# A macaron block on one core: the expert work of two more tiles moved behind the attention, and another chunk closed last

## The chip, the cores and the metric

The kernel runs on one core of a Trainium2 chip (trn2). The metric is the device time of one execution in microseconds. Every time below comes from the runs, from the page of one profiled execution or from its trace, whose clock starts at the first instruction.

## The reference

The input is `x`, 2048 rows of 128 float32 numbers. It goes through a feed-forward part, an attention part and the same feed-forward part again:

```python
x = x + 0.5 * ffn(layernorm(x))
x = x + attn(layernorm(x))        # 16 heads of 8, pages of 32 rows, causal by page, rope
x = x + 0.5 * ffn(layernorm(x))

def ffn(x):                       # L, N = 128, 16; eight experts, capacity 256 rows each
    y1 = ln(x + mha(x, ...), g1, b1)
    y2 = ln(y1 + moe(y1, ...), g2, b2)
    return y2

def moe(x):                       # softmax gate, best expert, rows beyond the capacity dropped
    h = einsum('ecd,edf->ecf', disp, w1) + b1
    y = einsum('ecf,efd->ecd', h, w2) + b2
    out = where(keep, gate_val * y[slot], 0)
```

There is no function between `w1` and `w2`, so the kernel folds each expert into one 128x128 matrix and applies all eight to every row; a coefficient per row and expert (the gate, or 0) picks the right one.

## The kernel before

**Tiles and chunks.** The 2048 rows are 16 tiles of 128 rows, in 4 chunks of 4 tiles. The engines are TensorE (PE), VectorE (DVE), ScalarE (ACT), GpSimd (POOL) and SyncE (SP). Every engine has its own instruction list, and semaphores (`wait_ge`, `then_inc`) tie them together. Nothing is scheduled by a planner: the order on each engine is written out by hand as words such as `P3` or `E10`, a step and the chunk or tile it is for.

**The steps of the second feed-forward part**, which the change is about: `O` adds the projected attention output to the rows and, with `X`, takes their statistics; `A` turns the rows; `P` multiplies them and takes the statistics of y1; `M` normalises y1 (DVE, L879); `C` turns y1 on PE and scales it on ACT and, in rows, on POOL (L545); `L` makes the gate's logits; `R` picks the expert (DVE, L794 to L813; PE, L1137 to L1141); `K` makes the coefficients (DVE, L820 to L823) and turns them; `B` adds a bias row (POOL L509, PE L1152, DVE L833). A letter with 0 to 3 is for a chunk.

**The expert step `E`** is for one tile, 0 to 15. PE makes two products of 512 columns, the high four experts and the low four (L1156, "two halves" below). ACT scales the high one (L673), DVE scales the low one and adds the high (L844, four instructions), and POOL adds the eight parts up in three instructions (L520, L525, L529). For tiles 14 and 15 the first of those three is on DVE (L851). PE may start the low half of tile t only when DVE has finished tile t - 2, since both use one bank:

```python
if t >= 2:
    pe.wait_ge(high_ready, k - 1)
experts(n, t, 1, t % 2)
if t >= 2:
    pe.wait_ge(pair_ready, k - 1)
experts(n, t, 0, 2 + t % 2)
```

**Closing a chunk.** `Z` takes the statistics of y2 (DVE L754 to L762, POOL L501), `V` normalises it on POOL (L535), `F` multiplies by the gain and adds the rows (for chunks 0 to 2 on POOL, `close`, L550 and L553; for chunk 3 on DVE, L958 and L965, four instructions each). SP then stores the chunk (L490).

**Early work.** The attention runs in 16 blocks (a chunk and four heads each). In it ACT does nothing but exponentials (L722), and PE does scores (L1325) and their products with the values (L1347). The steps of chunks 0 to 2 are threaded into these blocks by `PLAN`: `E8@12` in block 14 means the low half of tile 8 behind group 12 of that block, and `H8` is its high half, which DVE scales in place of ACT (L1041). `EARLY_POOL` is POOL's order for this. What is not in `PLAN` stands in the second entry of `ORDER`, and runs behind the last block: this is "the tail".

**Idle work.** `IDLE_WORK` puts products of a constant (L1162), whose result nobody reads, in front of a step on PE: `"C3": (0, 26)` is 26 of them ahead of `C3`.

Of the kernel before, what the change touches and what calls it, by code (L numbers as in the profile page):

```python
# [83 lines left out]
class Pass:  # L84
# [20 lines left out]
}  # L105
# [6 lines left out]
EARLY_POOL = ("X0 B0 P0 M0 C0 X1 B1 E0 P1 M1 C1 E1 E2 E3 Z0 V0 F0 X2 B2 E4 E5 P2 M2 C2 E6 E7 Z1 V1 F1 "  # L112
              "E8 E9")

# [21 lines left out]
    {  # L136
# [4 lines left out]
    },  # L141
# [3 lines left out]
START_WORK = 20  # L145
IDLE_WORK = {"C0": (12, 0), "O3": (0, 4), "A3": (0, 3), "C3": (0, 26), "L3": (0, 4),
             "K3": (0, 2), "B3": (0, 1)}
# [7 lines left out]
def build(nc, a, out):  # L155
    with ExitStack() as ctx:
# [52 lines left out]
        def rows(k):  # L209
# [115 lines left out]
        def group(g):  # L325
            return slice(GT * g, GT * (g + 1))
# [37 lines left out]
        def _(sp):  # L364
# [87 lines left out]
            with sp.If(beyond_safe > 0):  # L452
# [34 lines left out]
                sp.wait_ge(shift_out, 16 * 2 * G)  # L487
            for g in range(G):
                sp.wait_ge(x_new[2], g + 1)
                sp.dma_start(out[cols(g), :].rearrange("(t p) d -> p t d", p=P),  # L490
                             x_tm[:, GT * g:GT * (g + 1), :]).then_inc(stored, 16)
# [4 lines left out]
        def _(pool):  # L496
# [50 lines left out]
            def close(g):  # L547

                pool.wait_ge(normed[LN2], EARLY + g + 1)
                pool.tensor_tensor(y[:, group(g), :], y[:, group(g), :], rows_of(lnb[:, 0, :]), ALU.mult).then_inc(z_part, 1)  # L550
                pool.wait_ge(z_part, G + g + 1)
                pool.wait_ge(xb_ready, G + g + 1)
                pool.tensor_tensor(x_tm[:, group(g), :], y[:, group(g), :], xb[1][:, group(g), :],  # L553
                                   ALU.add).then_inc(x_new[2], 1)

# [3 lines left out]
            def feed_forward(n):  # L559
                for step, g in steps(n, "pool"):  # L560
# [10 lines left out]
                    elif step == "F":  # L571
                        close(g)
                    elif step == "D":

                        pool.wait_ge(const_in, 16 * SMALL)
                        pool.tensor_scalar(lnb[:], lnb[:], 0.5, None, ALU.mult).then_inc(prep_pool, 1)
                        pool.wait_ge(prep_pool, 2)
                    elif step == "B":
                        add_bias(n, g)
                    elif step == "b":  # L580
                        pool.wait_ge(b1_ready, 1)
                        pool.wait_ge(fold_in, 16 * FOLD)
# [165 lines left out]
        def _(dve):  # L748
# [108 lines left out]
            def feed_forward(n):  # L857
                for step, g in steps(n, "dve"):
# [87 lines left out]
                    elif step == "F":  # L946
# [7 lines left out]
                        else:  # L954
# [565 lines left out]
```

## Time and profile before

| | |
|---|---|
| median of 3 runs | 419.14 us (417.70 to 419.77) |
| the profiled execution | 418.99 us |
| its span in the trace, first to last instruction | 417.1 us |
| PE busy | 385.8 us (92%) |
| ACT busy | 325.8 us (78%) |
| DVE busy | 193.3 us (46%) |
| POOL busy | 129.4 us (31%) |
| exponentials of the attention on ACT (L722) | 253.4 us in 272 instructions |
| last exponential ends, tail begins | 381.1 us |
| last result instruction on DVE ends | 414.4 us |

The first 120 us are the first feed-forward part and the preparation of the attention, from 120 to 381 us the attention runs, and the rest is the tail. In the rows a time is the start from the beginning of the span, then the length in us, the engine, the line of the kernel and the operation with what it writes and reads; "x4" counts the instructions merged into the row; square brackets hold the idle time of the engine ahead of it and what ended it.

### The profile page before, as it was taken

The page shows a single profiled execution, that of the slowest core. Times are in us where ns is not written, and L with a number is a line of the kernel's source. Part 1 is how long each engine was busy: PE and PEld are TensorE (multiplying, and loading weights), DVE is VectorE, ACT ScalarE, POOL GpSimd, SP SyncE. Part 2 cuts the span into 40 slices and gives each one's busy share as a digit, 9 for nine tenths or more (in the row PEclk, how much of TensorE's full clock was granted, in tenths as well). Part 3 has the DMA queues.
Part 4 walks back from the last instruction along what each step waited for, and adds up shares of the span by engine and source line. Part 5 has one row for each costly group of instructions (what it writes and reads, how often), then busy time and mean ns, then how long its engine had stood idle before and what let it go on. Part 6 is the DMA issues. An engine that isn't in the chain of part 4 may idle for free.

```text
span 417.1 us, 7529 instructions
## 1 busy us (share of the span) xinstructions
PE 385.8 (92%) x2700; PEld 130.1 (31%) x2704; DVE 193.3 (46%) x729; ACT 325.8 (78%) x466; POOL 129.4 (31%) x203
## 2 busy tenths in 40 slices
PE   6889999789879999999999999999999999999991
PEld 3577443234322233222222222222222222213440
DVE  3866589799862333214242232261332421312856
ACT  1244556566789999999999999999999999996141
POOL 1372788673120023000302210063122330110594
PEclk9999999989988999999999999999999999999997
DMA  6891900000995399600000000000000000000001
GB/s 134 269 349 46 141 2 2 0 1 0 258 255 104 99 194 254 113 2 2 2 2 0 2 0 2 2 0 28 2 1 2 2 25 2 1 2 2 1 25 30
DMA packets 17758, 24.54 MB, mean 59 GB/s; under 512 B 2616, under 2 KB 14584, under 8 KB 16632
## 3 DMA queue, kind: packets, MB, share of 16 engines
q1 hardware_dynamic: 17428, 23.91, 23.9%
q8 instruction: 23, 0.38, 0.4%
q0 software_dynamic: 288, 0.10, 0.2%
q14 instruction: 19, 0.16, 0.1%
HBM read 16.60 MB, written 7.41 MB: 58 GB/s over the span
## 4 chain that ended last, share of the span: by engine, by line
PE 52%; ACT 15%; DVE 12%; issue 10%; DMA 4%; POOL 4%; SPq 1%; ACTq 0%; DVEq 0%; POOLq 0%
PE ps L1347 21%; ACT arena L722 13%; PE ps L1325 12%; PE ps L1156 8%; DVE stats L754 2%; PE ps L1094 2%; DVE arena L844 2%; DMA packed<-piece_dram 2%; PE ps L1110 2%; PE ps L1204 1%; PE ps L1130 1%; DMA x_tm<-in_x 1%; PE ps L1152 1%; DMA piece_dram<-packed 1%; POOL arena L520 1%
## 5 line engine op out<-in xcount | busy, mean ns | idle before, releaser
L722 ACT ACTIVATE arena<-ps 128x1024 f32<-128x1024 f32 x272 | 253.4, 1072 | 7.7 <-PE ps L1325 6.7
L1347 PE MATMUL ps<-arena,v_st 128*9 128x512 f32 (+3 forms) x1280 | 145.3, 536 | 0.1
L1325 PE MATMUL ps<-packed 51*128 51x512 bf16 (+4 forms) x640 | 94.5, 354 | 6.3 <-ACT arena L722 2.2
L501 POOL TENSOR_TENSOR rstd<-var_eps,neg_half 128x4 f32<-128x4 f32 x28 | 28.5, 1017 | 145.8 <-DVE var_eps L762 145.8
L1325 PEld LDWEIGHTS ps<-packed 51*128 51x128 bf16 (+1 forms) x640 | 23.8, 94 | 110.9 <-ACT arena L722 99.3
L1347 PEld LDWEIGHTS ps<-arena,v_st 128*9 128x9 f32 x1280 | 20.7, 89 | 52.6 <-issue 37.4
L520 POOL TENSOR_TENSOR arena<-trio 128x256 f32<-128x256 f32 x14 | 10.2, 726 | 86.7 <-DVE trio L844 86.7
L1156 PE MATMUL ps<-w,arena 128*128 128x512 f32 x64 | 31.0, 611 | 4.1 <-DVE arena L844 4.0
L1156 PE MATMUL ps<-w,trio 128*128 128x512 f32 x64 | 33.9, 629 | 0.0
L844 DVE SCALAR_TENSOR_TENSOR trio<-ps,arena,trio 128x128 f32<-128x128 f32 x64 | 18.0, 344 | 33.9 <-PE ps L1156 31.8
L989 DVE STREAM_TRANSPOSE o_t<-ps 128x512 f32<-128x512 f32 x16 | 11.5, 717 | 40.3 <-PE ps L1347 40.3
L673 ACT ACTIVATE arena<-ps,arena 128x128 f32<-128x128 f32 x64 | 17.9, 368 | 12.8 <-PE ps L1156 7.6
L1041 DVE TENSOR_SCALAR trio<-ps,arena 128x128 f32<-128x128 f32 x40 | 11.3, 345 | 26.1 <-PE ps L1156 26.1
L1162 PE MATMUL ps<-idle 128*128 128x512 bf16 x74 | 18.9, 400 | 2.8 <-DVE idle L973 2.5
L844 DVE SCALAR_TENSOR_TENSOR arena<-ps,arena 128x128 f32<-128x128 f32 x64 | 17.5, 342 | 3.5 <-ACT arena L673 1.9
L632 ACT ACTIVATE arena<-arena,offset,rstd 128x128 f32<-128x128 f32 x28 | 11.5, 484 | 9.7 <-POOL offset L504 9.7
L638 ACT ACTIVATE trio<-ps 128x512 f32<-128x512 f32 x9 | 5.4, 596 | 17.0 <-PE ps L1110 15.4
L1156 PEld LDWEIGHTS ps<-w,arena 128*128 128x128 f32 x64 | 10.9, 189 | 20.1 <-issue 10.3
L1156 PEld LDWEIGHTS ps<-w,trio 128*128 128x128 f32 x64 | 10.1, 188 | 21.7 <-issue 20.9
L545 POOL TENSOR_TENSOR arena<-arena,g_rep 128x512 f32<-128x512 f32 x8 | 10.1, 1272 | 21.7 <-PE ps L1110 21.7
L525 POOL TENSOR_TENSOR arena<-arena 128x128 f32<-128x128 f32 x32 | 15.7, 490 | 2.9 <-DVE arena L851 0.5
L529 POOL TENSOR_TENSOR arena<-arena 128x128 f32<-128x128 f32 x32 | 15.5, 483 | 2.5
(146 smaller groups left out, 404.9 us busy)
## 6 DMA issues: line engine op xcount, KB each, us to landing
packed<-piece_dram SPq DMA_DIRECT2D x16, 384.0 KB, 6.8
piece_dram<-packed SPq DMA_DIRECT2D x18, 256.0 KB, 4.0
packed<-in_w1T SPq DMA_DIRECT2D x8, 256.0 KB, 5.1
packed<-in_w SPq DMA_DIRECT2D x8, 256.0 KB, 5.5
trio<-in_rope SPq DMA_DIRECT2D x2, 1024.0 KB, 6.9
piece_dram<-trio SPq DMA_DIRECT2D x6, 256.0 KB, 9.8
packed<-in_template SPq DMA_DIRECT2D x2, 720.0 KB, 12.5
x_tm<-in_x SPq DMA_DIRECT2D x4, 256.0 KB, 5.8
```

Of the source, the lines that this page charges most:

```text
L501: pool.tensor_tensor(rstd[:, t], var_eps[:, t], neg_half[:], ALU.pow).then_inc(ln_rstd[kind], 1)
L520: pool.tensor_tensor(q, pair[n][:, t % 2, 0:2 * D], pair[n][:, t % 2, 2 * D:4 * D], ALU.add).then_inc(quad_ready, 1)
L525: pool.tensor_tensor(q[:, 0:D], q[:, 0:D], q[:, D:2 * D], ALU.add).then_inc(quad_ready, 1)
L529: pool.tensor_tensor(y[:, t, :], q[:, 0:D], base[:, t % (2 * GT), :], ALU.add).then_inc(z_ready, 1)
L632: ins = nc.scalar.activation(dst[:, t, :], src[:, t, :], ACT.Identity, bias=offset[:, t:t + 1], scale=rstd[:, t:t + 1])
L673: ins = nc.scalar.activation(prod[n][:, t % 2, cut], ps[:, t % 2, cut], ACT.Copy, scale=coef[n][:, t, e:e + 1])
L722: nc.scalar.activation(pexp[:, n % PB, :], ps[:, at:at + 2, :].rearrange("p b n -> p (b n)"), ACT.Exp, scale=SCALE).then_inc(run.exp_done, 1)
L844: ins = dve.scalar_tensor_tensor(pair[n][:, t % 2, D * e:D * (e + 1)], ps[:, bank, D * e:D * (e + 1)], coef[n][:, t, e:e + 1], prod[n][:, ...
L1156: pe.matmul(ps[:, bank, :], y1T[n][:, P * t:P * (t + 1)], w12[:, 512 * high:512 * (high + 1)], start=True, stop=True).then_inc(high_mm if ...
L1162: pe.matmul(ps[:, bank, :], idle[:, 0:P], idle[:], start=True, stop=True)
L1325: ins = pe.matmul(ps[:, 2 * (n % SLOTS) + b, col:col + w], tile_of(rows, 1, pair, j), packed[rows, c, 0, pair, q - GW * c:q - GW * c + w], ...
L1347: ins = pe.matmul(ps[32 * h:32 * h + VW, 6 + k % OB, q - GW * c:q - GW * c + w], v_st[:, j, GH * g + h, :], pexp[:, n % PB, 512 * b + col: ...
```

## The change

1. The four words `H8 E8 H9 E9` leave `PLAN`, and `E8 E9` leave `EARLY_POOL`. Tiles 8 and 9 get their expert work in the tail, whose orders are rewritten on PE, ACT, DVE and POOL. `E10` and `E11` are now ahead of `C3` on PE, and 12 idle products stand there in place of 26.
2. In the tail DVE takes the statistics `Z2` behind `K3` (it was behind `M3`), and POOL does `Z2 V2` behind `B3` (it was ahead of it).
3. POOL does `F2`, the closing of chunk 2, as its very last step; SP stores the chunks in the order 0, 1, 3, 2, the last one behind a semaphore `closing` of its own.
4. POOL waits for y1 of chunk 3 to be normalised (`M3`) before it adds up tile 9.

All lines of the functions move down by up to 7 (L1156 is L1163, L879 is L886).

```diff
@@ PLAN, EARLY_POOL
-    14: "Z1@0 L2@1 S2@5 R2@5 K2@7 B2@8 H8@10 E8@12", 15: "H9@1 E9@3",
+    14: "Z1@0 L2@1 S2@5 R2@5 K2@7 B2@8",
...
-              "E8 E9")
+              )
@@ ORDER, the tail
-        "pe": "E10 O3 A3 E11 P3 C3 L3 E12 R3 K3 E13 B3 E14 E15",
-        "act": "E10 A3 E11 C3 L3 K3 E12 E13 E14 E15",
-        "dve": "O3 X3 E10 P3 E11 M3 Z2 L3 R3 K3 E12 B3 E13 E14 E15 Z3 F3",
-        "pool": "X3 E10 P3 E11 C3 Z2 V2 F2 B3 E12 E13 E14 E15 Z3",
+        "pe": "E8 O3 A3 E9 P3 E10 E11 C3 L3 E12 R3 K3 E13 B3 E14 E15",
+        "act": "E8 A3 E9 E10 E11 C3 L3 K3 E12 E13 E14 E15",
+        "dve": "O3 X3 E8 P3 E9 M3 E10 E11 L3 R3 K3 Z2 E12 B3 E13 E14 E15 Z3 F3",
+        "pool": "X3 E8 P3 E9 E10 C3 E11 B3 Z2 V2 E12 E13 E14 E15 Z3 F2",
@@ IDLE_WORK
-IDLE_WORK = {"C0": (12, 0), "O3": (0, 4), "A3": (0, 3), "C3": (0, 26), "L3": (0, 4),
+IDLE_WORK = {"C0": (12, 0), "O3": (0, 4), "A3": (0, 3), "C3": (0, 12), "L3": (0, 4),
@@ SP
-            for g in range(G):
-                sp.wait_ge(x_new[2], g + 1)
+            for g in (0, 1, G - 1, EARLY - 1):
+                if g == EARLY - 1:
+                    sp.wait_ge(closing, 2)
+                else:
+                    sp.wait_ge(x_new[2], min(g, 2) + 1)
@@ POOL, close
+                part, at, closed = (closing, 1, closing) if g == EARLY - 1 else (z_part, G + g + 1, x_new[2])
                 pool.wait_ge(normed[LN2], EARLY + g + 1)
-                pool.tensor_tensor(y[:, group(g), :], y[:, group(g), :], rows_of(lnb[:, 0, :]), ALU.mult).then_inc(z_part, 1)
-                pool.wait_ge(z_part, G + g + 1)
+                pool.tensor_tensor(y[:, group(g), :], y[:, group(g), :], rows_of(lnb[:, 0, :]), ALU.mult).then_inc(part, 1)
+                pool.wait_ge(part, at)
@@ POOL, feed_forward
+                        if n and g == 9:
+                            pool.wait_ge(normed[LN1], 2 * G)
                         add_experts(n, g)
@@ DVE, F of the last chunk
-                            dve.wait_ge(z_part, q + 1)
+                            dve.wait_ge(z_part, q + 1 - n)
```

PE in the tail, from `P3` to `C3`, before: `P3` (L1094) is followed by the idle products and the turning of y1 (L1110).

```order
L1156 MATMUL ps<-w12,trio 128x512 [waits high_ready]
L1156 MATMUL ps<-w12,trio 128x512 [waits pair_ready]
L1094 MATMUL ps<-w_mha,trio 128x128 [waits copied_rows]
L1094 MATMUL ps<-w_mha,trio 128x128 x3
L1162 MATMUL ps<-idle 128x512 x26
L1110 MATMUL ps<-ident,arena 128x128 [waits normed_ln1]
```

The same place now:

```order
L1163 MATMUL ps<-w12,trio 128x512 [waits high_ready]
L1163 MATMUL ps<-w12,trio 128x512 [waits pair_ready]
L1101 MATMUL ps<-w_mha,trio 128x128 [waits copied_rows]
L1101 MATMUL ps<-w_mha,trio 128x128 x3
L1163 MATMUL ps<-w12,trio 128x512 [waits high_ready]
L1163 MATMUL ps<-w12,trio 128x512 [waits pair_ready]
L1163 MATMUL ps<-w12,trio 128x512 [waits high_ready]
L1163 MATMUL ps<-w12,trio 128x512 [waits pair_ready]
L1169 MATMUL ps<-idle 128x512 x12
L1117 MATMUL ps<-ident,arena 128x128 [waits normed_ln1]
```

The two halves ahead of `P3` are those of tile 9 (they were those of tile 11), and those of tiles 10 and 11 came in behind it; each half has its wait.

POOL in the tail, behind `C3`, before: `Z2` (L501, L504), `V2` (L535), `F2` (L550, L553), `B3` (L509), then tile 12.

```order
L545 TENSOR_TENSOR arena<-arena,g_rep 128x512 [waits turned_y1,normed_ln1]
L501 TENSOR_TENSOR rstd<-var_eps,neg_half 128x4 [waits ln_var_ln2]
L504 TENSOR_TENSOR offset<-neg_mean,rstd 128x4 [waits ln_rstd_ln2]
L535 TENSOR_SCALAR arena<-arena,rstd,offset 128x128 [waits ln_offset_ln2]
L535 TENSOR_SCALAR arena<-arena,rstd,offset 128x128 x3
L550 TENSOR_TENSOR arena<-arena,lnb 128x512 [waits normed_ln2]
L553 TENSOR_TENSOR x_tm<-arena 128x512 [waits xb_ready,z_part]
L509 TENSOR_TENSOR arena<-x_tm,lnb 128x512 [waits x_new_attn]
L520 TENSOR_TENSOR arena<-trio 128x256 [waits z_ready,pair_ready]
```

The same place now:

```order
L549 TENSOR_TENSOR arena<-arena,g_rep 128x512 [waits turned_y1,normed_ln1]
L524 TENSOR_TENSOR arena<-trio 128x256 [waits z_ready,pair_ready]
L529 TENSOR_TENSOR arena<-arena 128x128 [waits quad_ready]
L533 TENSOR_TENSOR arena<-arena 128x128 [waits quad_ready]
L513 TENSOR_TENSOR arena<-x_tm,lnb 128x512 [waits x_new_attn]
L505 TENSOR_TENSOR rstd<-var_eps,neg_half 128x4 [waits ln_var_ln2]
L508 TENSOR_TENSOR offset<-neg_mean,rstd 128x4 [waits ln_rstd_ln2]
L539 TENSOR_SCALAR arena<-arena,rstd,offset 128x128 [waits ln_offset_ln2]
L539 TENSOR_SCALAR arena<-arena,rstd,offset 128x128 x3
L524 TENSOR_TENSOR arena<-trio 128x256 [waits z_ready,pair_ready]
```

Tile 11 and `B3` now come ahead of `Z2 V2`, and `F2` is gone from here.

The end of POOL's list now (before, it ended with the first row but two, L501 there):

```order
L529 TENSOR_TENSOR arena<-arena 128x128 [waits last_quad]
L533 TENSOR_TENSOR arena<-arena 128x128 [waits quad_ready]
L505 TENSOR_TENSOR rstd<-var_eps,neg_half 128x4 [waits ln_var_ln2]
L555 TENSOR_TENSOR arena<-arena,lnb 128x512 [waits normed_ln2]
L558 TENSOR_TENSOR x_tm<-arena 128x512 [waits xb_ready,closing]
```

The two instructions of `F2` stand behind `Z3` (L505), which is what DVE's own last four instructions wait for.

## Rows read from the trace of the kernel before

**Rows 1.** The page, costliest groups: the exponentials on ACT.

```profile
L722 ACT ACTIVATE arena<-ps 128x1024 f32<-128x1024 f32 x272 | 253.4, 1072 | 7.7 <-PE ps L1325 6.7
```

**Rows 2.** Timeline of ACT, 318 to 381 us, the last two attention blocks.

```profile
350.60 3.77 ACT L722 ACTIVATE arena<-ps 128x1024 f32<-128x1024 f32 x4 [0.31 <-PE ps L1325]
354.69 10.38 ACT L722 ACTIVATE arena<-ps 128x1024 f32<-128x1024 f32 x11 [0.32 <-PE ps L1325]
365.39 15.69 ACT L722 ACTIVATE arena<-ps 128x1024 f32<-128x1024 f32 x17 [0.31 <-PE ps L1325]
```

**Rows 3.** Timeline of PE, 376 to 417 us, the tail.

```profile
386.69 1.88 PE L1156 MATMUL ps<-w,trio 128*128 128x512 f32 x4
388.41 1.05 PE L1094 MATMUL ps<-w_mha,trio 128*128 128x128 f32 x8
389.30 5.78 PE L1162 MATMUL ps<-idle 128*128 128x512 bf16 x25
395.49 0.66 PE L1110 MATMUL ps<-ident,arena 128*128 128x128 f32 x4 [0.41 <-DVE arena L879]
...
399.92 0.18 PE L1137 MATMUL ps<-pick_bf,tri_bf 128*128 128x32 bf16 x1
```

**Rows 4.** Timeline of DVE, 376 to 417 us, the tail.

```profile
390.67 0.87 DVE L754 BATCH_NORM_STATS2 stats<-arena 128x6 f32<-128x128 f32 x4
...
392.13 1.12 DVE L844 SCALAR_TENSOR_TENSOR trio<-ps,arena,trio 128x128 f32<-128x128 f32 x4
393.36 2.08 DVE L879 TENSOR_SCALAR arena<-arena,mv,rstd 128x128 f32<-128x128 f32 x4
...
399.57 0.20 DVE L811 TENSOR_TENSOR pick_bf<-arena,row_pick 128x32 bf16<-128x32 f32 x1
...
400.73 0.20 DVE L823 TENSOR_TENSOR arena<-pick,gate 128x32 f32<-128x32 f32 x1
402.86 1.13 DVE L844 SCALAR_TENSOR_TENSOR trio<-ps,arena,trio 128x128 f32<-128x128 f32 x4 [1.93 <-ACT trio L673]
...
413.25 1.14 DVE L965 SCALAR_TENSOR_TENSOR x_tm<-arena,rstd 128x128 f32<-128x128 f32 x4 [0.18 <-DVE arena L958]
```

**Rows 5.** Timeline of POOL, 376 to 417 us, the tail.

```profile
393.55 0.73 POOL L520 TENSOR_TENSOR arena<-trio 128x256 f32<-128x256 f32 x1
...
396.30 1.27 POOL L545 TENSOR_TENSOR arena<-arena,g_rep 128x512 f32<-128x512 f32 x1 [0.94 <-PE ps L1110]
...
399.13 1.76 POOL L535 TENSOR_SCALAR arena<-arena,rstd,offset 128x128 f32<-128x128 f32 x4
400.98 1.26 POOL L550 TENSOR_TENSOR arena<-arena,lnb 128x512 f32<-128x512 f32 x1
...
403.55 1.26 POOL L509 TENSOR_TENSOR arena<-x_tm,lnb 128x512 f32<-128x512 f32 x1
404.77 0.72 POOL L520 TENSOR_TENSOR arena<-trio 128x256 f32<-128x256 f32 x1
...
406.52 0.72 POOL L520 TENSOR_TENSOR arena<-trio 128x256 f32<-128x256 f32 x1
...
410.57 0.45 POOL L529 TENSOR_TENSOR arena<-arena 128x128 f32<-128x128 f32 x1
412.11 1.05 POOL L501 TENSOR_TENSOR rstd<-var_eps,neg_half 128x4 f32<-128x4 f32 x1 [1.09 <-DVE var_eps L762]
```

**Rows 6.** Timelines of POOL and DVE, 335 to 338 us: a large and a small instruction together.

```profile
336.17 1.27 POOL L553 TENSOR_TENSOR x_tm<-arena 128x512 f32<-128x512 f32 x1
...
336.48 1.01 DVE L811 TENSOR_TENSOR pick_bf<-arena,row_pick 128x32 bf16<-128x32 f32 x1
```

**Rows 7.** DMA issues, 400 to 417 us: the two last stores, KB each, us to landing.

```profile
out_rows<-x_tm SPq DMA_DIRECT2D x2, 256.0 KB, 2.3
```

**Rows 8.** Busy time by stretch: PE, PEld, DVE, ACT, POOL, then PEclk, DMA share, GB/s.

```profile
80.00:82.00 2.00, 0.11 (x1) 0.00 (x0) 1.93 (x13) 0.00 (x0) 0.21 (x1) 1.00 0.00 0
...
84.00:86.00 2.00, 1.48 (x3) 0.37 (x2) 2.00 (x7) 0.86 (x3) 1.92 (x3) 0.50 0.00 0
```

More of the change, by code:

```diff
@@ L276, in build @@
         wo_in = sem("wo_in")
+        closing = sem("closing")
         const_in, mha_in, route_in, fold_in, att_in, rope_in, template_in = (sem(n) for n in
@@ L547, in close @@
             def close(g):
+                part, at, closed = (closing, 1, closing) if g == EARLY - 1 else (z_part, G + g + 1, x_new[2])
                 pool.wait_ge(normed[LN2], EARLY + g + 1)
-                pool.tensor_tensor(y[:, group(g), :], y[:, group(g), :], rows_of(lnb[:, 0, :]), ALU.mult).then_inc(z_part, 1)
-                pool.wait_ge(z_part, G + g + 1)
+                pool.tensor_tensor(y[:, group(g), :], y[:, group(g), :], rows_of(lnb[:, 0, :]), ALU.mult).then_inc(part, 1)
+                pool.wait_ge(part, at)
                 pool.wait_ge(xb_ready, G + g + 1)
                 pool.tensor_tensor(x_tm[:, group(g), :], y[:, group(g), :], xb[1][:, group(g), :],
-                                   ALU.add).then_inc(x_new[2], 1)
+                                   ALU.add).then_inc(closed, 1)
             pool.memset(neg_half[:], -0.5).then_inc(prep_pool, 1)
```

## The prediction

> **What bounds the kernel now.** I read the page first, for the engine that is busy longest, then the timeline of ACT through the attention, then the timelines of PE, DVE and POOL in the tail side by side. The attention belongs to ACT: its 272 exponentials are 253.4 us, and it stands idle for 7.7 us in all, nearly always for a score product of PE [rows 1]. The reader is to see that ACT never waits long, but a little at a time, behind each piece of early work on PE [rows 2]. The tail is another kernel: no engine is full, and what counts is one chain through them. PE multiplies (`P3`), DVE takes statistics and normalises, PE turns y1 as soon as DVE is done (395.49, idle until L879) [rows 3], and so on to the last adds on POOL and DVE's last four instructions [rows 4, 5]. I make the sum against the profiled execution, 418.99 us, which is 0.15 us under the median of 419.14 us. A difference of 0.5%, 2.1 us, is about what a measurement of this kernel can tell from none.
>
> **1. Four expert halves leave the attention: -1.6 us.** ACT's free pace is that of its last run, 17 exponentials in 15.69 us, the last of them 1.07 long: (15.69 - 1.07) / 16 = 0.91 us each. The four from 350.60 to 354.69 took 4.09 us in place of 3.64, 0.45 lost; the eleven from there to 365.39 took 10.70 in place of 10.01, 0.69 lost [rows 2]. The idle gap ahead of 350.60 is like the one ahead of 354.69, 0.45 again. These are exactly the places of `H8`, `E8`, `H9` and `E9`: 1.6 us. Bounds: 1.2 us (the four idle gaps alone, at 0.31) and 1.9.
>
> **2. The same work in the tail is hidden in itself.** Tile 8 and 9 stand where tiles 10 and 11 stood. Tiles 10 and 11 are 2 x 1.88 us on PE (the row at 386.69) [rows 3] in place of 14 of the 26 idle products; on DVE they are 2 x 1.1 us where `Z2` stood. `Z2`, 1.5 us (390.67 to 392.13) [rows 4], goes into the 1.93 us in which DVE waited for ACT (402.86) [rows 4]. That costs nothing as long as the waits fit, and one doesn't.
>
> **3. `C3` comes late: +1.3 us.** PE may start the low half of tile 11 only when DVE has finished tile 9, and DVE does tile 9 behind `P3`, in the slot that ends at 393.25 (392.13 + 1.12) [rows 4]. PE gets there long before: it begins the last pass of `P3` at about 389.2 and three halves are 3 x 0.86, so it stands from about 392.1 to 393.3. Then come the low half, 0.9, and 12 idle products at 0.22 (5.78 us for about 26 [rows 3]), 2.6 us: PE can turn y1 at 396.8, not at 395.5. Queued behind that wait on PE are `C3`, `L3` and all that follows. DVE's normalising will be faster, since POOL's adds no longer run beside it: four instructions took 2.08 us beside them (393.36 and 393.55) [rows 4, 5], and four instructions of that size by themselves, L844, take 1.12. It ends between 394.2 and 394.5, I take 394.2, and I count the gain at nothing, because PE is not ready before 396.8.
>
> **4. DVE's pick meets POOL: +0.85 us.** One row shows what a long POOL add does to a small DVE instruction with two inputs in SBUF: L811, 0.20 us when free [rows 4], took 1.01 us and ended just behind POOL's L553 [rows 6]. POOL in the tail now does three tiles and `C3` on end from 394.2: 3 x 1.75 (404.77 to 406.52) [rows 5] + 1.27 = 6.5 us, so `B3`, 1.26 us (403.55) [rows 5], runs from 400.7 to 402.0. DVE's L811 is due at 399.57 + 1.3 = 400.9, inside it. It will end at 402.1 and not at 401.1. PE had 0.15 us to spare there (tile 12 held it until 399.92 [rows 3]), so 0.85 us go through. Bounds: 0, if POOL is 0.4 us later than I have it, and 1.2.
>
> The Trainium skill, "SBUF — State Buffer", section "Who interferes with whom", says that DVE with two SBUF inputs and GpSimd reading SBUF exclude each other for a whole instruction; that row agrees. By its rule the DVE instructions of the expert step, with one input in PSUM, are untouched.
>
> **5. The last adds: +0.3 us.** `K3` ends on DVE at 400.93 + 2.15 = 403.1, then `Z2` until 404.6, POOL's `Z2 V2` 3.1 us (1.05 at 412.11 and 1.76 at 399.13 [rows 5], and 0.3 for the small one and the gaps) until 407.8, then tiles 12 and 13 at 1.75 and 14 and 15 at 1.0: 413.3. Tile 15 ended at 411.02 before (410.57 + 0.45) [rows 5], 413.2 with terms 3 and 4. So POOL, idle at this place before, is just full, and DVE's two adds L851 now meet it. I take 0.3; bounds 0 and 1.
>
> **6. `F2` stands bare at the end: +2.4 us.** Until now it was done at 403.6, beside other work. Behind POOL's L501 (end 413.16) DVE needed 1.23 us to the last row of the output (413.25 + 1.14). Now POOL has two instructions of 1.26 us behind L501 as well, 2.6 us with a gap: 1.4 us more even if nobody disturbs anybody. And DVE's four instructions read two SBUF tensors each, like L811, so I let them take turns with POOL: 1.26 + 1.05 + 1.27 = 3.6 us, 2.4 more than before. The upper bound is 3.3: if the two chunks finish together, SP's stores, of which one needs 2.3 us to land [rows 7], queue up, which I estimate from that row at under half of it, 0.9. What follows the last row is otherwise as before, 417.1 - 414.4 = 2.7 us.
>
> No row of before has these four instructions beside a POOL add. By the same rule of the Trainium skill ("SBUF — State Buffer") they exclude each other, which favours 2.4 over 1.4.
>
> **Sum:** -1.6 + 1.3 + 0.85 + 0.3 + 2.4 = +3.25, so 418.99 + 3.2 = **422.2 us**.
>
> **Rival A, not slower: no turns.** POOL and DVE don't meet, neither at L811 nor at the end. For it: POOL's place is a sum over seven instructions, and 0.4 us later sets L811 free; L811 beside the shorter POOL instructions of 399 us was not held [rows 4, 5]. Against: rows 6. Then -1.6 + 1.3 + 0.3 + 1.4 = +1.4, **420.4 us**, within 0.5%. It decides as soon as both overlaps cost under 1 us together.
>
> **Rival B: PE keeps pace.** The wait for tile 9 is not felt, because DVE finishes it before `P3` or I have misread PE's place. Then 12 idle products end at 395.4, `C3` is where it was, terms 3 to 5 vanish and only `F2` is left: -1.6 + 1.4 = **418.8 us**. Against it speaks DVE's written order.
>
> **Rival C, faster: only the attention counts.** `F2` too is covered, and the faster normalising comes through by 1.0 us: -1.6 - 1.0, **416.4 us**. It needs B and a POOL that is nowhere the last, which the 3.1 us of `Z2 V2` speak against.
>
> **Rival D: TensorE's clock falls in the tail.** PE was busy for 0.11 us in 80 to 82 us, and at 84 to 86 its granted clock was 0.50, the 1.2 GHz level [rows 8]. The new standstill is 1.2 us among full work, so I think it is not enough. If it is, the low half and the idle products, 3.5 us, take twice that: **425.7 us**.
>
> That term 1 does not appear (the change doing nothing in the attention) would give 423.8 us; it is inside the range.
>
> **How the numbers follow.** Forecast 0.50 (0.45 of it slower by over 0.5%, 0.05 just under), A 0.20, B 0.15, C 0.10, D 0.05. Slower: 0.45 + 0.05 = 0.50. Within 0.5%: 0.05 + A + B = 0.40. Faster: C, 0.10. The range leaves out C, D and the far end of the bounds: from 418.3, under B, to 424.0, which is the sum with `F2` at 3.3 and the last adds at 1. The likeliest case by itself has 421.2 to 424.0.
>
> **What would show it.** In the profile after: ACT's idle in the attention down by about 1.2 us; PE idle for about 1.2 us ahead of a low half some 12 us behind the last exponential; the turning of y1 15.7 us behind the end of the last exponential (now 395.49 - 381.08 = 14.4); L818 (now L811) near 1 us long with POOL's L513 beside it; POOL without idle time from `Z2` to tile 15; L555 and L558 behind everything. If the turning of y1 comes no later than 14.4 us behind the last exponential, or if L972 is over before L558 begins by more than 1 us with both at their old lengths, term 3 or 6 is wrong and the time is under 421.

## The result and the profile after

| | before | after |
|---|---|---|
| median of 7 runs each, us | 418.86 (416.86 to 419.77) | 422.12 (420.36 to 423.63) |
| ratio, with its 95% interval | | 1.0088 [1.0065, 1.0112] |
| the profiled execution, and its span | 418.99, 417.1 | 423.63, 421.8 |
| first exponential of the attention at | 120.24 | 122.05 |
| attention, first to end of last exponential | 260.84 | 258.65 |
| tail, end of last exponential to end of span | 36.01 | 41.13 |

The changed kernel is slower: by 0.9% by the ratio, and by 3.3 us by the two medians. The profiled execution of after is the slowest of its seven: it came to the first exponential 1.8 us later, where the two programs are the same. So I count every place of the tail from the end of the last exponential, 381.08 us before and 380.70 after, and call that point X. An instruction that takes longer than its usual length because another engine's runs beside it is called held below.

Below stand the page of after, costliest groups, the row that answers to [rows 1]; and the timeline of ACT in the attention, 318 to 381 us, which answers to [rows 2].

```profile
L729 ACT ACTIVATE arena<-ps 128x1024 f32<-128x1024 f32 x272 | 252.7, 1093 | 5.9 <-PE ps L1332 5.0
```

```profile
336.50 44.20 ACT L729 ACTIVATE arena<-ps 128x1024 f32<-128x1024 f32 x48
```

The idle time of ACT fell from 7.7 to 5.9 us, and the last 48 exponentials are one unbroken row of 44.20 us. Before, three gaps stood in them [rows 2]; the first of their four rows begins at 335.43, and the same 48 took 381.08 - 335.43 = 45.65.

```profile
335.43 14.87 ACT L722 ACTIVATE arena<-ps 128x1024 f32<-128x1024 f32 x16
```

The timeline of PE in the tail, after; columns as in [rows 3], at the end in brackets the idle time ahead and who ended it.

```profile
392.93 1.13 PE L1163 MATMUL ps<-w,trio 128*128 128x512 f32 x2 [1.27 <-DVE trio L851]
393.89 2.75 PE L1169 MATMUL ps<-idle 128*128 128x512 bf16 x12
396.48 0.60 PE L1117 MATMUL ps<-ident,arena 128*128 128x128 f32 x4
```

PE stands for 1.27 us until DVE has finished tile 9, begins the low half of tile 11 at 392.93, 12.2 us behind X, runs the 12 idle products and turns y1 at 396.48, 15.78 us behind X (14.41 before). The reader should compare this with the timeline of DVE, which answers to [rows 4]: y1 was normalised at 392.98 + 1.11 = 394.09 and lay there for 2.4 us.

```profile
391.75 1.12 DVE L851 SCALAR_TENSOR_TENSOR trio<-ps,arena,trio 128x128 f32<-128x128 f32 x4
392.98 1.11 DVE L886 TENSOR_SCALAR arena<-arena,mv,rstd 128x128 f32<-128x128 f32 x4
...
400.54 0.19 DVE L818 TENSOR_TENSOR pick_bf<-arena,row_pick 128x32 bf16<-128x32 f32 x1
400.65 1.30 DVE L820 TENSOR_TENSOR pick<-arena,row_pick 128x32 f32<-128x32 f32 x1
...
404.30 1.13 DVE L851 SCALAR_TENSOR_TENSOR trio<-ps,arena,trio 128x128 f32<-128x128 f32 x4 [0.22 <-issue]
...
415.04 3.16 DVE L972 SCALAR_TENSOR_TENSOR x_tm<-arena,rstd 128x128 f32<-128x128 f32 x4 [0.18 <-DVE arena L965]
```

The timeline of POOL, which answers to [rows 5]:

```profile
400.64 1.27 POOL L513 TENSOR_TENSOR arena<-x_tm,lnb 128x512 f32<-128x512 f32 x1
404.16 1.02 POOL L505 TENSOR_TENSOR rstd<-var_eps,neg_half 128x4 f32<-128x4 f32 x1 [2.25 <-DVE var_eps L769]
...
412.35 0.45 POOL L533 TENSOR_TENSOR arena<-arena 128x128 f32<-128x128 f32 x1
413.90 1.05 POOL L505 TENSOR_TENSOR rstd<-var_eps,neg_half 128x4 f32<-128x4 f32 x1 [1.09 <-DVE var_eps L769]
414.93 1.26 POOL L555 TENSOR_TENSOR arena<-arena,lnb 128x512 f32<-128x512 f32 x1
416.26 1.26 POOL L558 TENSOR_TENSOR x_tm<-arena 128x512 f32<-128x512 f32 x1
```

Two places are to be read across the engines. At 400.64 POOL's L513 and DVE's L820, both with two inputs in SBUF, begin within 0.01 us: the short one lasts 1.30 us in place of 0.2. At 414.93 and 416.26 POOL's two instructions of `F2` stand beside DVE's last four, which last 3.16 us in place of 1.14 [rows 4].

The DMA issues of the last stores, 404 to 422 us, which answer to [rows 7]:

```profile
out_rows<-x_tm SPq DMA_DIRECT2D x2, 256.0 KB, 2.6
```

They are issued 37.52 and 37.95 us behind X, 0.43 us apart. Before, the one of chunk 2 had gone at 22.53, 10.8 us ahead of the last.

### The profile page after: what moved, and what is told of

Same layout as the page of the kernel before. It is cut to its first block, busy times and chain, and to the rows that moved or that the text cites. A ratio compares the mean times of both kernels' runs of the same rounds, so it can differ in the third digit from the quotient of the medians.

```text
span 421.8 us, 7505 instructions
## 1 busy us (share of the span) xinstructions
PE 386.2 (92%) x2690; PEld 131.4 (31%) x2690; DVE 193.0 (46%) x721; ACT 327.2 (78%) x474; POOL 128.7 (31%) x203
## 3 DMA queue, kind: packets, MB, share of 16 engines
q1 hardware_dynamic: 17428, 23.91, 23.6%
## 4 chain that ended last, share of the span: by engine, by line
PE 48%; ACT 18%; issue 12%; DVE 11%; POOL 5%; DMA 2%; SPq 1%; DVEq 0%; ACTq 0%; POOLq 0%
PE ps L1354 18%; ACT arena L729 15%; PE ps L1332 11%; PE ps L1163 7%; PE ps L1101 2%; DVE stats L761 2%; PE ps L1211 2%; DVE arena L851 2%; PE ps L1137 2%; PE ps L1117 1%; DMA x_tm<-in_x 1%; DMA piece_dram<-packed 1%; POOL arena L524 1%; POOL arena L533 1%; POOL arena L529 1%
## 5 line engine op out<-in xcount | busy, mean ns | idle before, releaser
L1332 PE MATMUL ps<-packed 51*128 51x512 bf16 (+4 forms) x640 | 95.5, 352 | 7.5 <-ACT arena L729 2.5
L505 POOL TENSOR_TENSOR rstd<-var_eps,neg_half 128x4 f32<-128x4 f32 x28 | 28.5, 1017 | 177.6 <-DVE var_eps L769 177.6
L1163 PE MATMUL ps<-w,arena 128*128 128x512 f32 x64 | 31.0, 611 | 4.1 <-DVE arena L851 4.0
L1163 PE MATMUL ps<-w,trio 128*128 128x512 f32 x64 | 33.3, 625 | 1.3 <-DVE trio L851 1.3
L851 DVE SCALAR_TENSOR_TENSOR trio<-ps,arena,trio 128x128 f32<-128x128 f32 x64 | 17.9, 343 | 26.1 <-PE ps L1163 25.4
L1169 PE MATMUL ps<-idle 128*128 128x512 bf16 x64 | 17.3, 415 | 2.5 <-DVE idle L980 2.5
L851 DVE SCALAR_TENSOR_TENSOR arena<-ps,arena 128x128 f32<-128x128 f32 x64 | 17.5, 341 | 3.5 <-ACT arena L680 3.1
L1048 DVE TENSOR_SCALAR trio<-ps,arena 128x128 f32<-128x128 f32 x32 | 9.0, 344 | 20.0 <-PE ps L1163 20.0
L1163 PEld LDWEIGHTS ps<-w,arena 128*128 128x128 f32 x64 | 10.9, 189 | 20.1 <-issue 10.3
L549 POOL TENSOR_TENSOR arena<-arena,g_rep 128x512 f32<-128x512 f32 x8 | 10.1, 1271 | 22.3 <-PE ps L1117 22.3
L1163 PEld LDWEIGHTS ps<-w,trio 128*128 128x128 f32 x64 | 10.3, 189 | 21.3 <-issue 18.5
```

Source lines behind the costliest of these rows:

```text
L505: pool.tensor_tensor(rstd[:, t], var_eps[:, t], neg_half[:], ALU.pow).then_inc(ln_rstd[kind], 1)
L851: ins = dve.scalar_tensor_tensor(pair[n][:, t % 2, D * e:D * (e + 1)], ps[:, bank, D * e:D * (e + 1)], coef[n][:, t, e:e + 1], prod[n][:, ...
L1163: pe.matmul(ps[:, bank, :], y1T[n][:, P * t:P * (t + 1)], w12[:, 512 * high:512 * (high + 1)], start=True, stop=True).then_inc(high_mm if ...
L1169: pe.matmul(ps[:, bank, :], idle[:, 0:P], idle[:], start=True, stop=True)
L1332: ins = pe.matmul(ps[:, 2 * (n % SLOTS) + b, col:col + w], tile_of(rows, 1, pair, j), packed[rows, c, 0, pair, q - GW * c:q - GW * c + w], ...
```

## The experiments

The table has the places of all kernels, each in us behind its own X: y1 turned, last row of `K3` on DVE, tile 15 added up, last row of the output, end of the span; and the duration of DVE's last four instructions. "Single" stands for one time alone, which has no ratio. The ratio is to the kernel before in the same session, whose median was 418.95 us for e1, e3, e4 and e5, 418.58 for e2, e6, e7 and e8, and 417.92 for e9 to e12.

| kernel | median us (n) | ratio [95%] | y1 turned | K3 | tile 15 | last four | last row | end |
|---|---|---|---|---|---|---|---|---|
| before | 418.86 (7) | | 14.41 | 19.85 | 29.94 | 1.14 | 33.31 | 36.01 |
| after | 422.12 (7) | 1.0088 [1.0065, 1.0112] | 15.78 | 21.78 | 32.11 | 3.16 | 37.50 | 41.13 |
| e1_f2_last | 421.73 (4) | 1.0076 [1.0047, 1.0106] | 14.42 | 19.89 | 29.98 | 3.16 | 35.38 | 39.00 |
| e5_no_halves | 417.57 (10) | 0.9969 [0.9950, 0.9987] | 14.42 | 19.87 | 29.97 | 1.14 | 33.34 | 36.03 |
| e4_f2_memset | 420.02 (1) | single | 15.78 | 21.33 | 31.68 | 1.14 | 35.05 | 38.68 |
| e3_b3_early | 421.75 (4) | 1.0077 [1.0047, 1.0107] | 15.78 | 21.18 | 31.49 | 3.16 | 36.88 | 40.52 |
| e12_after_again | 422.40 (1) | single | 15.78 | 21.78 | 32.10 | 3.16 | 37.49 | 41.12 |
| e2_no_idle | 420.99 (10) | 1.0059 [1.0035, 1.0082] | 13.45 | 20.12 | 30.47 | 3.16 | 35.87 | 39.50 |
| e6_e9_first | 421.16 (1) | single | 14.25 | 20.65 | 31.01 | 3.16 | 36.40 | 40.02 |
| e7_idle1_b3 | 420.41 (1) | single | 13.45 | 20.11 | 30.46 | 3.16 | 35.86 | 39.49 |
| e11_idle32 | 422.13 (1) | single | 15.13 | 21.69 | 31.78 | 1.14 | 35.15 | 37.85 |
| e8_spread | 419.40 (12) | 1.0009 [0.9987, 1.0030] | 13.46 | 20.04 | 30.99 | 1.14 | 34.36 | 37.06 |
| e9_split_f2 | 417.69 (12) | 0.9990 [0.9967, 1.0013] | 13.44 | 19.42 | 30.36 | 1.14 | 33.73 | 36.43 |
| e10_e11_late | 417.25 (12) | 0.9982 [0.9964, 1.0000] | 13.45 | 18.86 | 30.29 | 1.14 | 33.65 | 36.35 |

The time from the span's start to the first exponential ranged from 119.35 to 122.64 us over these executions, in code that none of them changes. That is why a single time says less here than the places. Most of this spread goes with TensorE's granted clock, read over 0 to 118 us: the mean is 1.00 in e1 and 0.99 in e2 and before (119.35 to 120.24 us), 0.97 in seven others (six of them at 120.28 to 120.89, e8 at 122.64), and 0.96 in e5, e9, e11 and after (121.41 to 122.26).

The attention can be read in the same way, from the first exponential to X, with the mean granted clock of 118 to 150 us, where its only stretches at the 1.2 GHz level lie:

| kernel | halves in the attention | granted clock, 118 to 150 us | attention, us |
|---|---|---|---|
| before | yes | 0.89 | 260.84 |
| e1, e11 | yes | 0.95 | 260.12, 260.08 |
| after and the nine others | no | 0.95 | 258.6 to 258.7 |
| e2 | no | 1.00 | 258.05 |

At equal clock the halves cost 1.4 to 1.5 us, and each 0.05 of this mean goes with 0.6 to 0.7 us, with the halves and without. That the clock is the cause is read from these rows; no experiment changed it alone.

### e1: `F2` last and nothing else

The kernel before with that part of the change alone.

```diff
@@ before: SP's order and close() as in the change
-        "pool": "X3 E10 P3 E11 C3 Z2 V2 F2 B3 E12 E13 E14 E15 Z3",
+        "pool": "X3 E10 P3 E11 C3 Z2 V2 B3 E12 E13 E14 E15 Z3 F2",
```

> The kernel before with nothing changed but the place of F2 (last on POOL, chunk 2 stored last). My theory: POOL's two instructions and DVE's last four take turns behind L501, the two stores queue up, and the 2.5 us that POOL saves earlier buy nothing, because tile 15 waits for DVE there: the tail (last exponential to the end of the span) goes from 36.0 to 38.9 us, the time up by 2.9 us. DVE's last four last 3.2 us and not 1.1. Rival: POOL's earlier time is worth something and DVE and POOL run side by side at the end: up by 1.4 us or less.

The timelines of DVE and POOL at the end, of this kernel:

```profile
412.02 3.16 DVE L970 SCALAR_TENSOR_TENSOR x_tm<-arena,rstd 128x128 f32<-128x128 f32 x4 [0.18 <-DVE arena L963]
```

```profile
411.90 1.26 POOL L555 TENSOR_TENSOR arena<-arena,lnb 128x512 f32<-128x512 f32 x1
413.24 1.26 POOL L558 TENSOR_TENSOR x_tm<-arena 128x512 f32<-128x512 f32 x1
```

Everything up to tile 15 is where it was; the tail is 39.00 - 36.01 = 2.99 us longer. Of this 2.07 are up to the last row (35.38 for 33.31) and 0.92 behind it (39.00 - 35.38 = 3.62, before 2.70), where two stores now leave together. The DMA packets of the two stores show it: before, those of the last store take 1.04 us from first to last, here those of both take 1.96. Term 6 stands alone, with its mechanism.

### e5: the four halves left out of the attention

Before, without the expert products of tiles 8 and 9, whose values are then not computed.

```diff
@@ before: PE, early
+                elif i in (8, 9):
+                    pe.sem_inc(high_mm if step == "H" else low_mm, 1)
```

> The kernel before, in which PE leaves out the four products of tiles 8 and 9 in the attention and only counts their semaphores up; all the rest stays (left out: the expert products of tiles 8 and 9). My theory of term 1: ACT's starts are 0.90 us apart through blocks 14 and 15 but for the bias product, the attention is 1.7 us shorter, the tail stays at 36.0 us, the time falls by 1.7 us. Rival: ACT is bound by itself there and the gaps are taken up elsewhere: less than 0.5 us.

The timeline of ACT in the attention, 318 to 382 us:

```profile
336.66 44.19 ACT L722 ACTIVATE arena<-ps 128x1024 f32<-128x1024 f32 x48
```

It is the row of after, 44.20, to 0.01 us. The tail did not move (36.03). The 48 exponentials are 1.45 us shorter than before, where I had expected 1.7, and by the ratio the kernel is 0.3% faster, 1.3 us. So term 1 is in the early products of PE alone.

### e4: memsets in place of `F2`'s multiply and add

After; chunk 2's last multiply and add are left out.

```diff
@@ after: close, chunk 2
-                pool.tensor_tensor(y[:, group(g), :], y[:, group(g), :], rows_of(lnb[:, 0, :]), ALU.mult)
+                pool.memset(y[:, group(g), :], 1.0)
...
-                pool.tensor_tensor(x_tm[:, group(g), :], y[:, group(g), :], xb[1][:, group(g), :], ALU.add)
+                pool.memset(x_tm[:, group(g), :], 1.0)
```

> The kernel after, with the two instructions of F2 replaced by memsets of the same 128x512 (left out: chunk 2's last multiply and add). A memset writes SBUF and reads nothing. If DVE's last four were long because POOL's instructions read SBUF beside them, they go back from 3.16 to about 1.14 us. If they were long because the two engines write to SBUF, or because of the semaphores, they stay near 3 us for as long as the memsets run.

The timeline of both engines, 412 to 416 us:

```profile
413.31 0.52 POOL L556 MEMSET arena<- 128x512 f32 x1
413.44 1.14 DVE L978 SCALAR_TENSOR_TENSOR x_tm<-arena,rstd 128x128 f32<-128x128 f32 x4 [0.18 <-DVE arena L971]
413.89 0.53 POOL L562 MEMSET x_tm<- 128x512 f32 x1
```

POOL writes the same bytes to SBUF at the same moment and reads none, and DVE's four are 1.14 again. So what holds them is POOL's reading, not its writing or its being busy.

In this execution the pick that `K3` uses was free, too. The timelines of DVE and POOL, 396 to 404 us:

```profile
399.50 0.18 DVE L826 TENSOR_TENSOR pick<-arena,row_pick 128x32 f32<-128x32 f32 x1
```

```profile
399.49 1.32 POOL L513 TENSOR_TENSOR arena<-x_tm,lnb 128x512 f32<-128x512 f32 x1
```

POOL's L513 begins 0.01 us ahead of it, as in after, yet DVE went first, and `K3` ended 0.45 us earlier. Whether after is held there each time was open, hence e12.

### e12: after, unchanged

> The kernel after once more, unchanged. In its first profile L820 was held for 1.1 us by POOL's L513, which began 10 ns before it. If that is a race between two instructions that come within hundredths of a microsecond, another execution has L820 at 0.18 us, K3 at 21.2 to 21.4 us in place of 21.8 and the tail at 40.5 to 40.7 us; if it is a fixed order, all is as in the first profile (21.8, 41.1).

The timelines of DVE and POOL:

```profile
399.42 1.31 DVE L820 TENSOR_TENSOR pick<-arena,row_pick 128x32 f32<-128x32 f32 x1
```

```profile
399.41 1.27 POOL L513 TENSOR_TENSOR arena<-x_tm,lnb 128x512 f32<-128x512 f32 x1
```

Held again, and all places agree with the first profile to 0.01 us. Two of two executions of after were held, the one of e4 was not. POOL began 0.01 us ahead in all three; in e4 its L513 took 1.32 us in place of 1.27, as if there POOL had been the one to wait. What decides it can't be read from the starts, and stays open.

### e3: `B3` ahead of `P3` on POOL

```diff
@@ after
-        "pool": "X3 E8 P3 E9 E10 C3 E11 B3 Z2 V2 E12 E13 E14 E15 Z3 F2",
+        "pool": "X3 E8 B3 P3 E9 E10 C3 E11 Z2 V2 E12 E13 E14 E15 Z3 F2",
```

> The kernel after with POOL's B3 moved from behind E11 into its idle time ahead of P3. My theory of term 4: DVE's L820 (1.30 us, ended with POOL's L513) goes back to 0.2 us, K3 ends 0.56 us earlier in the tail (21.2 in place of 21.8 us behind the last exponential), and the whole tail is 0.4 to 0.6 us shorter, as Z2 and POOL's last adds hang on K3. Rival: L820 stays long, because it isn't B3 that holds it, and the tail stays at 41.1 us.

The timelines of DVE and POOL:

```profile
399.06 0.18 DVE L820 TENSOR_TENSOR pick<-arena,row_pick 128x32 f32<-128x32 f32 x1
```

```profile
388.63 1.27 POOL L513 TENSOR_TENSOR arena<-x_tm,lnb 128x512 f32<-128x512 f32 x1
```

`K3` ends 0.60 us earlier and the span 0.61. That is what term 4 is worth, 0.6 and not 0.85. The medians (421.75 and 422.12) can't show it.

### e2: no idle products ahead of `C3`

```diff
@@ after
-IDLE_WORK = {"C0": (12, 0), "O3": (0, 4), "A3": (0, 3), "C3": (0, 12), "L3": (0, 4),
+IDLE_WORK = {"C0": (12, 0), "O3": (0, 4), "A3": (0, 3), "C3": (0, 0), "L3": (0, 4),
```

> The kernel after without the 12 idle products ahead of C3. My theory: they stand behind the wait for tile 9 and run while y1 is already there, so PE turns y1 2.3 us earlier, 13.4 us behind the last exponential (15.8 in the kernel after). From there Z2 becomes the bound, since it waits for POOL to finish tile 11 at 20.0 us: tile 15 ends on POOL 1.9 us earlier (30.2), the tail is 39.2 us and the time 1.9 us less than that of the kernel after. Rival: the idle products hold the granted clock up and without them the products of the tail are slow: no gain, and a granted clock of 0.5 in the tail.

The timeline of PE, and the busy time by stretch around its standstill (columns as in [rows 8]):

```profile
389.62 1.12 PE L1163 MATMUL ps<-w,trio 128*128 128x512 f32 x2 [1.26 <-DVE trio L851]
390.85 0.66 PE L1117 MATMUL ps<-ident,arena 128*128 128x128 f32 x4
```

```profile
388.00:392.00 4.00, 2.64 (x11) 1.07 (x10) 3.86 (x19) 1.54 (x5) 2.27 (x4) 1.00 0.00 0
```

The granted clock stays at 1.00, the 2.4 GHz level, through a stretch in which PE is busy for 2.64 of 4 us; rival D has no support. y1 is turned 2.33 us earlier, yet `K3` only 1.66. Timelines of DVE and POOL:

```profile
394.41 1.29 DVE L812 SCALAR_TENSOR_TENSOR arena<-arena,rank 128x32 f32<-128x32 f32 x1
```

```profile
394.38 1.26 POOL L549 TENSOR_TENSOR arena<-arena,g_rep 128x512 f32<-128x512 f32 x1
```

With everything earlier, another pair has met: POOL's rows of `C3` (L549) hold L812 of the pick. I had not expected that, and the tail is 39.50 us where I had expected 39.2.

### e6 and e7: tile 9 earlier on DVE, and e2 with e3

```diff
@@ e6: after
-        "dve": "O3 X3 E8 P3 E9 M3 E10 E11 L3 R3 K3 Z2 E12 B3 E13 E14 E15 Z3 F3",
+        "dve": "O3 X3 E8 E9 P3 M3 E10 E11 L3 R3 K3 Z2 E12 B3 E13 E14 E15 Z3 F3",
@@ e7: after with the pool order of e3, and
-             "C3": (0, 12)
+             "C3": (0, 1)
```

> The kernel after with DVE doing tile 9 ahead of P3 and not behind it. PE's wait ahead of the low half of tile 11 vanishes, P3 on DVE starts 0.5 us later. My theory: the 12 idle products now end at 14.3 us behind the last exponential, y1 is turned at 14.4 us (15.8), and the tail is 1.3 us shorter, 39.8 us. Rival: P3's delay of 0.5 us passes through everything: the tail 0.5 us longer, 41.6 us.

> The kernel after with B3 early on POOL and one idle product ahead of C3. If the two terms stand apart, the tail falls by 1.9 + 0.6 us to 38.6 us. If POOL's chain from the normalised y1 through tile 11, Z2, V2 and tiles 12 to 15 is what holds it once C3 is early, B3 has left this chain's middle already with no more to give than the wait of Z2 allows: 39.2 us, with y1 turned at 13.4 us.

The timeline of PE in e6:

```profile
387.47 3.60 PE L1163 MATMUL ps<-w,trio 128*128 128x512 f32 x8
390.90 2.54 PE L1169 MATMUL ps<-idle 128*128 128x512 bf16 x11
393.49 0.60 PE L1117 MATMUL ps<-ident,arena 128*128 128x128 f32 x4
```

The eight products run without the standstill, and y1 is turned 1.53 us earlier: the wait of term 3 is the order of `P3` and `E9` on DVE. The tail gains 1.10, less than y1, since L549 holds L812 here too (1.07 us). e7 ends at 39.49, as e2 does at 39.50: once y1 is early, moving `B3` gives nothing, since L549 again holds L812 (396.13, 1.28 us, beside 396.11, 1.26 us). The gains of e2 and e3 do not add.

### e11: before, with `C3` delayed alone

```diff
@@ before
-             "C3": (0, 26)
+             "C3": (0, 32)
```

> The kernel before with 32 idle products ahead of C3 in place of 26. PE then turns y1 1.0 us later (15.4 us behind the last exponential; 14.4), with nothing else changed. My theory of term 3: a late C3 passes through in full, tile 15 ends at 30.9 us (29.9) and the tail is 37.0 us (36.0). Rival: the chain behind it has room, and the tail grows by less than 0.4 us.

The timelines of PE, DVE and POOL:

```profile
390.57 7.07 PE L1162 MATMUL ps<-idle 128*128 128x512 bf16 x32
397.47 0.60 PE L1110 MATMUL ps<-ident,arena 128*128 128x128 f32 x4
```

```profile
402.74 1.29 DVE L823 TENSOR_TENSOR arena<-pick,gate 128x32 f32<-128x32 f32 x1
```

```profile
402.72 1.26 POOL L550 TENSOR_TENSOR arena<-arena,lnb 128x512 f32<-128x512 f32 x1
```

Six more idle products turned y1 0.72 us later (I had expected 1.0), and the tail grew by 1.84: the 0.72 in full, and 1.1 because the last step of `K3` now runs into POOL's `F2`. So before sits in a gap between such meetings: 0.72 us of delay is enough to leave it.

### e8, e9, e10: the halves out of the attention, the tail put in order

All three keep what the change takes out of the attention and store the chunks in the order 0 to 3. e8 does `F2` on DVE behind `E13`, and `V2` on ACT; in e9 POOL does the add of `F2`, and waits for `K3`'s coefficients before its rows of `C3`; e10 also holds tile 11's adds on POOL until the pick is done.

```diff
@@ e8: after, with `C3` idle (0, 1), and F of chunk 2 on DVE
+        "act": "E8 A3 E9 E10 E11 C3 L3 K3 E12 E13 V2 E14 E15",
+        "dve": "O3 X3 E8 P3 E9 M3 E10 E11 L3 R3 K3 Z2 E12 B3 E13 F2 E14 E15 Z3 F3",
+        "pool": "X3 E8 B3 P3 E9 E10 E11 C3 Z2 E12 E13 E14 E15 Z3",
@@ e9: on top
+        "pool": "X3 E8 B3 P3 E9 E10 E11 C3 Z2 E12 E13 F2 E14 E15 Z3",
+                        if n:
+                            pool.wait_ge(coef_ready, 2 * G)
                         scale_rows(n, g)
@@ e10: on top
+                        if n and g == 11:
+                            pool.wait_ge(pick_ready, 4 * G)
```

> A version meant to keep the change's gain in the attention and undo each loss in the tail: one idle product ahead of C3, B3 on POOL ahead of P3, V2 on ACT (behind tile 13), F2 on DVE (between tiles 13 and 14), C3's rows behind tile 11 on POOL, chunks stored in order. My theory: y1 turned at 13.4 us, tile 15 done on POOL at 29.0 us (before: 29.9), DVE's last four 1.14 us long, tail 35.1 us (before: 36.0), attention 1.7 us shorter: 2.6 us less than before. Rival: the work on ACT and DVE is in the way of tiles 12 to 15 and the tail is no shorter than before: 1.7 us less or worse.

> The spread version, in which F2 on DVE (one add 1.10 us long beside a POOL add) and C3's rows on POOL (beside which DVE's coefficients took 0.80 us) cost what was won. Here F2's multiply is on DVE between tiles 13 and 14, its add on POOL behind tile 13, and C3's rows wait for K3. My theory, that nearly all that is lost there is DVE and POOL excluding each other: K3 0.6 us earlier (19.4), tile 15 done at 29.9 us in place of 31.0, tail 36.0 us, the time 1.3 to 1.8 us under that of the kernel before. Rival: DVE is simply full behind K3, so the tail stays at 37.0 us and the time at that of before.

> The same with POOL's adds of tile 11 waiting until DVE has picked the expert. DVE's L809 there took 0.74 us beside them; it goes back to 0.2, K3 ends at 18.9 to 19.4 us. Against that Z2 gets tile 11 later (19.9 us). My theory: tail 0.3 to 0.6 us shorter than with the early tile 11, 35.5 us. Rival: Z2's wait gives it all back, tail 36.0 us.

e8, timelines of DVE and of POOL:

```profile
398.38 0.74 DVE L809 SCALAR_TENSOR_TENSOR arena<-arena,rank 128x32 f32<-128x32 f32 x1
...
400.60 0.80 DVE L827 TENSOR_TENSOR arena<-pick,gate 128x32 f32<-128x32 f32 x1
...
407.20 1.10 DVE L957 TENSOR_TENSOR x_tm<-arena 128x512 f32<-128x512 f32 x1
```

```profile
398.35 0.72 POOL L521 TENSOR_TENSOR arena<-trio 128x256 f32<-128x256 f32 x1
...
400.09 1.26 POOL L546 TENSOR_TENSOR arena<-arena,g_rep 128x512 f32<-128x512 f32 x1
```

POOL's three-part adds of tile 11 (L521) hold L809, its rows of `C3` (L546) hold L827, and a third meeting holds DVE's add L957 of `F2`. They cost what the new places should have given: I had expected a tail of 35.1 us and a time 2.6 us under before, the tail is 37.06, and e8 equals before. In e9 POOL's wait for the coefficients frees the last step of `K3` (19.42 us behind X, as expected), but tile 15 is at 30.36 and the tail at 36.43, where I had expected 29.9 and 36.0, and the 1.3 to 1.8 us under before did not come: the ratio is 0.9990, no difference. In e10 the second wait frees L809's counterpart, L816. Its timeline of DVE:

```profile
395.97 0.18 DVE L816 SCALAR_TENSOR_TENSOR arena<-arena,rank 128x32 f32<-128x32 f32 x1
...
397.64 0.19 DVE L834 TENSOR_TENSOR arena<-pick,gate 128x32 f32<-128x32 f32 x1
...
403.09 1.26 DVE L961 TENSOR_TENSOR arena<-arena,lnb 128x512 f32<-128x512 f32 x1
...
405.43 1.27 DVE L862 TENSOR_TENSOR arena<-trio 128x256 f32<-128x256 f32 x1
```

`K3` now ends 18.86 us behind X, 1 us earlier than before. Then tile 15 gives it back (30.29, before 29.94): `Z2` and half of `F2` are now in front of it, that half (L961) is held by POOL's adds of tile 13 (1.26 us, in e9 0.68), and L862 is held by POOL's add of `F2` (405.16, 1.26 us). e10 is the fastest of all: 0.9982 of before, 0.7 us, with an interval whose upper end is 1.0000, so at most a hair faster, and by the two ratios 1% under after. Its tail is 36.35 us where I had expected 35.5. By the places, 1.45 less in the attention and 0.34 more in the tail should leave 1.1 us.

## Why the prediction was right

**1, the halves leave the attention** (-1.6): -1.45 over the last 48 exponentials, confirmed alone by e5. The lower bound of 1.2 us counted four idle gaps, but rows 2 show three, 0.94 us together. The sign on ACT's idle time was 1.2 us; it was 1.8 over the whole attention, which holds the difference of the clock too.

**2, tiles 8 and 9 and `Z2` hidden** (0): DVE's L851 of tile 12 had 1.93 us of idle time ahead of it [rows 4] and now has 0.22, so `Z2` just fits in. Tile 12 is 23.6 us behind X (404.30), before 21.8 (402.86): 1.8 later, less than `K3`.

**3, `C3` late** (+1.3): +1.37, with the predicted wait (1.27 us, for DVE's tile 9). The early normalising was worth 1 us, ending 13.39 us behind X for 14.35, and as said was not felt. e6 shows whose order makes the wait, e2 that it and the idle products held y1; e11 shows on before that a late y1 passes in full.

**4, the pick meets POOL** (+0.85): here size and place were off. The step "DVE's L811 is due at 399.57 + 1.3 = 400.9, inside it" failed: that instruction (now L818) took 0.19 us, just ahead of POOL, and the next with two inputs in SBUF, L820, was held for 1.30. L820 does not stand between PE and the pick, only in front of `K3`, and so passes less: `K3` is 0.56 later than `C3` explains, e3 gives 0.60. That this pair met at all was narrow: in e4 it went the other way.

**5, last adds** (+0.3): tile 15 is 2.17 us later than before, `K3` 1.93, so 0.24. POOL had no idle time from 404.16 to the end of tile 15, as said.

**6, `F2` bare at the end** (+2.4): the last row is 4.19 us later, of which 2.02 are left for this term, where the taking of turns was put at 2.4. From the end of L505 (414.95) DVE needed 3.25 us, not 3.6: I had put the turns at 1.26, 1.05 and 1.27 us, the middle one from no row, and they came out as 1.29, 1.34 and 0.52, since the last two of DVE's four instructions ran through once POOL was done. The rows of the chain of waits of after, at its end (start, length, what):

```profile
415.04 1.29 DVE x_tm L972
416.33 1.34 DVEq L156
417.67 0.52 DVE x_tm L972 x2
```

What I had kept for the upper bound, that the stores queue up (0.9), did happen: 3.63 us from the last row to the end, before 2.70. Together 2.95. The step that failed is "What follows the last row is otherwise as before, 417.1 - 414.4 = 2.7 us": the packets of the two stores now follow one another, 1.96 us from first to last in place of 1.04. SP stores chunk 3 first, whose rows end at 418.20, though POOL has chunk 2 ready at 417.52. Whether the other order would give part of the 0.9 back was not tested.

The tail's terms were to give +4.85 and gave +5.12. With -1.45 that is +3.7; the ratio says +3.7 of 418.86, the medians say +3.3, and the spans, with 2.19 less in the whole attention, +2.9 without the part ahead of it. The 0.7 us between 2.19 and 1.45 is attention that the change doesn't touch: the profiled execution of before had a granted clock of 0.89 in 118 to 150 us, after 0.95, and e1 and e11, with the halves and 0.95, took 260.1 us and not 260.8.

That 422.12 came within 0.1 us of 422.2 is in part luck. Term 4 was 0.3 us too high and term 6 0.55 too low, and the sum started from 418.99 us, where the median of seven is 418.86. What the prediction had right is the list of places, their signs and most of the sizes. The range's upper end is a slip of 0.2: with `F2` at 3.3 and the last adds at 1 the sum gives 423.8, not 424.0.

**The rivals.** A (no turns) falls with the 3.16 us of after and e1; it was right only about L818. B (PE keeps pace) falls with PE's 1.27 us. C falls with both. D: no stretch of 2 us from 386 to 398 of after has a granted clock under 1.00, and from 388 to 404 e2 has none either. That e1 and e3, each with only some of the terms, are as slow as after within their intervals shows that the times alone would not have told the forecast from half of it; the places do.

**The rule on the two engines.** Every hold above but that of the normalising has DVE instructions with two SBUF inputs on one side and a reading POOL instruction on the other. The Trainium skill, "SBUF — State Buffer", section "Who interferes with whom", states this as a lock for a whole instruction. This case agrees, with 1.30 for 0.19 and 3.16 for 1.14 us, and the memsets of e4 agree from the other side.

Not every such pair is held here, though. Before, DVE's L823 (two SBUF inputs, 0.20 us at 400.73) [rows 4] and L813 (0.18 us at 399.70) ran at their usual length inside POOL's L535, four TENSOR_SCALAR instructions that read SBUF (399.13 to 400.89) [rows 5]. And in after L965, DVE's four instructions ahead of the last four, took 1.13 us from 413.73 beside POOL's L505 (413.90, 1.05 us), a TENSOR_TENSOR of 4 elements per partition. All holds seen are beside POOL's TENSOR_TENSOR of 128 to 512 elements.

## What to carry to other kernels

A closing step that was hidden in the middle of a tail is not free at its end: count its own length, the neighbour that it will now meet, and the store that can no longer go early, here 3 us against 1.5 won in the attention. Two instructions that must not meet can't be kept apart by an order that is right to 1 us; most re-orderings here made a new pair meet, and what did part two pairs was a wait on the engine with slack (e9, e10). Where a gain is smaller than the spread of a part that is not changed, read the places relative to the last common event.

## What was not expected of the hardware

- DVE and POOL instructions that meet are sensitive to 0.01 us: L820 beside L513 took 1.3 us in two executions of after, and 0.18 in e4, where POOL was again ahead by 0.01 us.
- One long POOL instruction holds one DVE instruction, whatever the length of that: 0.19 us ones (L812, L820, L823) end 1.28 to 1.31 us after their start beside a POOL instruction of 1.26 or 1.27. In e8 L809 took 0.74 beside a POOL add of 0.72, and L827, begun in the middle of one of 1.26, took 0.80: each ends just behind POOL's.
- DVE's normalising, which has one input in SBUF and scalars, is slowed too: its four instructions took 2.08 us beside POOL's adds [rows 4, 5] and 1.11 without them.
- Two stores of 256 KB issued 0.43 us apart have packets for 1.96 us from first to last, one alone for 1.04 (before), so hardly any of the two runs side by side, and the end comes 0.9 us later behind the last row.
- POOL gives way too: L513 took 1.30 us in e2, where DVE's last step of `K3` had begun 0.03 us ahead of it, and 1.32 in e4.
